# A decoder layer on one core: the quantised MLP's transposes by TensorE or by DMA

## The reference

```python
x = x + attn(ln(x))      # causal, 8 query heads, 2 key/value heads of 128 from latents of 32, softmax, wo
x = x + xattn(ln(x), ctx) # 16 heads of 16 over 77 keys, then relu(out @ W1 + b1) @ W2 + b2, 256 -> 512 -> 256
x = x + ffn(ln(x))       # 256 -> 1024 -> 256, quantised
...
scale = 127.0 / jnp.clip(jnp.max(jnp.abs(x), axis=-1, keepdims=True), EPS, None)   # per row, behind an rmsnorm
return jnp.clip(jnp.round(x * scale), -128, 127) / scale
...
scale = 1.0 / jnp.clip(jnp.mean(jnp.abs(w)), EPS, None)                            # one for the matrix
return jnp.clip(jnp.round(w * scale), -1, 1) / scale
...
h = gelu(bitlinear(x, w1, b1)); return bitlinear(h, w2, b2)
```

## Time and profile before

| | |
|---|---|
| three runs | 325.93, 327.07, 327.6 us; median 327.07 |
| the profiled execution | 328.01 us |
| its span (first to last instruction) | 326.2 us |
| mean granted TensorE clock | 0.99 |

### The profile page before, as it was taken

How to read it: one execution, slowest core, us unless ns; L and a number is a source line. 1 busy time by engine, 2 the same in 40 slices (tenths; PEclk the granted TensorE clock), 3 DMA queues, 4 the chain that set the end, 5 groups by cost and what they waited for, 6 DMA issues and landing times.

```text
span 326.2 us, 8843 instructions
## 1 busy us (share of the span) xinstructions
PE 304.7 (93%) x3174; PEld 242.7 (74%) x3174; DVE 271.5 (83%) x488; ACT 188.9 (58%) x367; POOL 162.0 (50%) x315
## 2 busy tenths in 40 slices
PE   0999889999999999999999999999999999999956
PEld 0578668688876897888877876888878786887634
DVE  1058987877878998999999989899999898899973
ACT  0434317335564674477746962798278636967762
POOL 7044158049118518740684078512760376457781
PEclk9999999999999999999999999999999999999987
DMA  7999000000000000001000000000010010000001
GB/s 204 342 368 301 3 1 2 2 2 0 2 4 2 1 2 2 1 2 34 0 3 20 4 16 0 2 2 1 3 34 2 2 34 2 18 1 2 19 33 64
DMA packets 11732, 12.54 MB, mean 38 GB/s; under 512 B 1639, under 2 KB 10729, under 8 KB 11690
## 3 DMA queue, kind: packets, MB, share of 16 engines
q1 hardware_dynamic: 10698, 11.66, 11.1%
q10 hardware_dynamic: 992, 0.33, 0.5%
HBM read 9.89 MB, written 2.10 MB: 37 GB/s over the span
## 4 chain that ended last, share of the span: by engine, by line
PE 66%; DVE 17%; POOL 7%; issue 5%; DMA 2%; ACT 1%; SPq 1%; DVEq 0%; POOLq 0%; ACTq 0%
PE bank L1872 7%; PE bank L1702 7%; PE bank L1782 6%; PE bank L1881 5%; PE bank L1849 5%; PE bank L1800 4%; PE bank L1708 3%; PE bank L1863 3%; PE quad L1762 3%; PE bank L1901 3%; PE quad L1839 3%; PE bank L1920 3%; PE bank L1696 2%; DVE c_nm L1251 2%; DVE c_s L1262 2%
## 5 line engine op out<-in xcount | busy, mean ns | idle before, releaser
L824 ACT ACTIVATE c_p<-bank 77x512 f32<-77x512 f32 x64 | 35.9, 589 | 34.6 <-PE bank L1849 34.3
L1849 PE MATMUL bank<-ident,c_s 128*77 128x128 f32 x256 | 37.1, 278 | 0.4 <-DVE a_y L1229 0.2
L579 POOL TENSOR_SCALAR f_s<-f_s 128x1 f32<-128x1 f32 x16 | 3.7, 229 | 66.8 <-ACT f_sq L870 53.9
L1849 PEld LDWEIGHTS bank<-ident,c_s 128*77 128x77 f32 x256 | 29.1, 147 | 4.9 <-issue 2.1
L800 ACT ACTIVATE a_p<-bank 128x512 f32<-128x512 f32 x48 | 26.9, 597 | 9.4 <-PE bank L1782 9.2
L1872 PE MATMUL bank<-c_y,xw_s 128*128 128x128 f32 x256 | 31.5, 276 | 0.2 <-DVE c_y L1281 0.2
L1872 PEld LDWEIGHTS bank<-c_y,xw_s 128*128 128x128 f32 x256 | 30.4, 192 | 1.4 <-issue 0.5
L1881 PE MATMUL bank<-xw_s,c_h 128*128 128x256 f32 x128 | 30.7, 383 | 0.0
L1251 DVE TENSOR_REDUCE c_nm<-quad 128x16 f32<-128x1232 f32 x16 | 22.9, 1431 | 4.8 <-PE quad L1839 4.8
L1320 DVE SCALAR_TENSOR_TENSOR f_h<-bank,f_s,fb_s 128x512 f32<-128x512 f32 x32 | 22.9, 739 | 3.7 <-PE bank L1901 3.3
L1881 PEld LDWEIGHTS bank<-xw_s,c_h 128*128 128x128 f32 x128 | 23.1, 190 | 3.4 <-issue 0.8
(11 more groups left out here) (138 smaller groups left out, 746.3 us busy)
## 6 DMA issues: line engine op xcount, KB each, us to landing
out<-f_o SPq DMA_DIRECT2D x16, 128.0 KB, 1.7
xres<-in_x SPq DMA_DIRECT2D x1, 1536.0 KB, 10.1
c_p<-in_wqT SPq DMA_DIRECT2D x2, 512.0 KB, 6.6
c_p<-in_wo SPq DMA_DIRECT2D x1, 1024.0 KB, 9.2
f_h<-in_fw1T SPq DMA_DIRECT2D x1, 1024.0 KB, 12.2
c_s<-in_fw2T SPq DMA_DIRECT2D x1, 1024.0 KB, 11.3
xw_s<-in_xw SPq DMA_DIRECT2D x2, 512.0 KB, 9.9
xres<-in_x SPq DMA_DIRECT2D x2, 256.0 KB, 5.4
```

Of the source, the lines that this page charges most:

```text
L824: nc.scalar.activation(c_p[0:M, :, qt * P:(qt + 1) * P].rearrange("p (c j g) t -> p c j g t", c=KC, g=Q2)[:, :, j, :, :], bank("xs", f"tr{ ...
L1849: last = nc.tensor.transpose(dst[0:M, g * P:(g + 1) * P], c_s[:, qt, j, g, :], ident[:, :])
```

## The change

The rounded tiles get a second copy in bfloat16, f_qb and f_hb, written by ScalarE (f1_qb, f2_hb) from SBUF with 1536 taken off. For elements 0 to 6 (BY_DMA = 7) SyncE then transposes them by DMAs into f_qT and f_hT, one DMA for each 128x128 block, 2 for a tile of f_q and 8 for a tile of f_hq; TensorE's and ScalarE's f1_qT and f2_hT are gone for these elements, and their fills of the rotating banks with them. For element 7 TensorE transposes the bfloat16 copy, and ScalarE evacuates it as before. SyncE's list has the transposes and the stores in an order written by hand. x of element 0 moves to ScalarE's queue; the context is loaded in two halves with a semaphore each, behind the first value weights. The tables and the calls of all engines are in a new order.

```diff
         def _(sp):
-            sp.dma_start(xres[:, 0:TT, :], xin[:, 0:TT, :]).then_inc(ld_x0, 16)
-            sp.dma_start(ctxa[:, :], ctxT[0:P, :]).then_inc(ld_ctx, 16)
-            sp.dma_start(ctxb[:, :], ctxT[P:P + CK, :]).then_inc(ld_ctx, 16)
-            sp.dma_start(xk_a[:, :], xk[0:P, :]).then_inc(ld_ctx, 16)
-            sp.dma_start(xk_b[:, :], xk[P:P + CK, :]).then_inc(ld_ctx, 16)
+            @element
+            def f1_qT(i, t):
+                sp.wait_ge(*f1.after("act", f"qb{t}", i))
+                for n in range(2 * t, 2 * t + 2):
+                    sp.wait_ge(*f1.after("pe", f"l1_{n}", i - 1))
+                for c in range(KC):
+                    sp.dma_start(f_qT[:, c, t * P:(t + 1) * P], f_qb[:, t, c * P:(c + 1) * P], transpose=True).then_inc(tr_q[t], 16)
+            @element
+            def f2_hT(i, t):
+                sp.wait_ge(*f2.after("act", f"hb{t}", i))
+                sp.wait_ge(*f2.after("pe", f"l2{t}", i - 1))
+                for c in range(FC):
+                    sp.dma_start(f_hT[:, t, c, :], f_hb[:, t, c * P:(c + 1) * P], transpose=True).then_inc(tr_h[t], 16)
...
             sp.dma_start(xv_a, xv[0:P, :]).then_inc(ld_xv, 16)
+            sp.dma_start(ctxa[:, 0:KH], ctxT[0:P, 0:KH]).then_inc(ld_ctx[0], 16)
             sp.dma_start(xv_b, xv[P:P + CK, :]).then_inc(ld_xv, 16)
+            sp.dma_start(ctxb[:, 0:KH], ctxT[P:P + CK, 0:KH]).then_inc(ld_ctx[0], 16)
+            sp.dma_start(xk_a[:, :], xk[0:P, :]).then_inc(ld_xk, 16)
+            sp.dma_start(xk_b[:, :], xk[P:P + CK, :]).then_inc(ld_xk, 16)
+            sp.dma_start(ctxa[:, KH:2 * KH], ctxT[0:P, KH:2 * KH]).then_inc(ld_ctx[1], 16)
+            sp.dma_start(ctxb[:, KH:2 * KH], ctxT[P:P + CK, KH:2 * KH]).then_inc(ld_ctx[1], 16)
             sp.dma_start(wkup_s[:, :], wkupT).then_inc(ld_up, 16)
...
-            for i in range(B):
-                for t in range(TT):
-                    sp.wait_ge(*f2.after("dve", f"out{t}", i))
-                    sp.dma_start(xout[:, i * TT + t, :], f_o[:, t, :]).then_inc(out_sem[t], 16)
...
+            f1_qT(2, 1)
+            f2_store(0, 0)
+            f2_hT(1, 1)
+            f2_store(0, 1)
+            f1_qT(3, 1)
+            f2_hT(1, 0)
+            f1_qT(3, 0)
...
+            f1_qT(6, 0)
+            f1_qT(6, 1)
+            f2_hT(5, 0)
+            f2_store(4, 0)
+            f2_hT(5, 1)
+            f2_hT(6, 0)
+            f2_store(4, 1)
+            f2_hT(6, 1)
+            f2_store(5, 0)
+            f2_store(5, 1)
...
         def _(act):
+            def transposed(done, n, i):
+                if i >= 0:
+                    act.wait_ge(done, 16 * n * min(i + 1, BY_DMA))
...
+            @element
+            def f2_hb(i, t):
+                act.wait_ge(*f2.after("dve", f"hq{t}", i))
+                transposed(tr_h[t], FC, i - 1)
+                if i > BY_DMA:
+                    act.wait_ge(*f2.after("pe", f"hT{t}", i - 1))
+                nc.scalar.activation(f_hb[:, t, :], f_hq[:, t, :], ACT.Copy, bias=-ROUND16).then_inc(f2.sem["act"], 1)
...
+            act.dma_start(xres[:, 0:TT, :], xin[:, 0:TT, :]).then_inc(ld_x0, 16)
...
             def f2_hq(i, t):
...
-                dve.wait_ge(*f2.after("pe", f"hT{t}", i - 1))
+                dve.wait_ge(*f2.after("act", f"hb{t}", i - 1))
...
             def f2_l2(i, t):
...
-                pe.wait_ge(*f2.after("act", f"hT{t}", i))
+                if i < BY_DMA:
+                    pe.wait_ge(tr_h[t], 16 * FC * (i + 1))
+                else:
+                    pe.wait_ge(*f2.after("act", f"hT{t}", i))
```

More of the change, by code:

```diff
@@ new lines, in _ @@
+            xp_q(4)
+            f2_hb(1, 1)
+            f1_gelu(2, 0)
+            f1_gelu(2, 1)
+            f1_pre(1)
+            sa_exp(5, "B", 0)
+            f2_ssq(2, 1)
+            sp_q(6)
+            xm_relu(3, 1)
+            sa_exp(5, "B", 3)
+            sa_exp(5, "B", 2)
+            xs_exp(4, 0, 3)
+            xs_exp(4, 0, 1)
+            f2_ssq(2, 0)
+            f2_hb(1, 0)
+            xs_exp(4, 1, 3)
+            xs_exp(4, 1, 1)
+            xs_exp(4, 1, 0)
+            sa_exp(5, "A", 0)
@@ L1044, in _ @@
+            sa_exp(5, "B", 1)
+            xs_exp(4, 1, 2)
+            xs_exp(4, 0, 2)
+            xs_exp(4, 0, 0)
+            f1_qb(3, 1)
+            sp_v(6)
+            f1_qb(3, 0)
+            sa_exp(6, "A", 1)
+            f1_pre(2)
+            f2_hb(2, 1)
+            xm_relu(4, 1)
+            f1_gelu(3, 1)
+            xm_relu(4, 0)
+            sp_xT(7)
             f1_pre(3)
-            xm_relu(3, 0)
-            xp_q(4)
-            f1_gelu(2, 0)
+            xp_xT(5)
+            f2_ssq(3, 1)
@@ L1147, in _ @@
-            f1_qT(6, 0)
+            xs_exp(7, 0, 1)
+            xs_exp(7, 1, 2)
             xs_exp(7, 1, 0)
-            xs_exp(7, 1, 2)
             xs_exp(7, 1, 1)
+            f1_qb(6, 0)
             xs_exp(7, 1, 3)
+            f1_pre(6)
+            f2_hb(5, 0)
+            f1_gelu(5, 1)
+            xm_relu(7, 0)
+            f1_qb(6, 1)
             f1_pre(7)
-            xm_relu(7, 0)
+            f2_ssq(5, 1)
             f1_gelu(6, 0)
+            xm_relu(7, 1)
+            f2_hb(5, 1)
@@ L1170, in _ @@
+            f2_hb(7, 1)
             f2_hT(7, 0)
@@ L1565, in _ @@
             xo_T(4, 1)
             xo_y(4, 1)
+            so_resid(5)
+            f1_q(3, 0)
+            xp_ln(5)
+            xo_y(4, 0)
+            f1_h(3, 3)
+            f2_hq(2, 0)
+            f1_h(3, 2)
+            sa_max(6, "B")
+            f2_hmax(3, 1)
+            xm_resid(4, 1)
+            f1_h(3, 1)
+            f1_h(3, 0)
+            sa_sub(6, "B", 0)
+            f1_ln(4, 1)
+            xm_resid(4, 0)
+            sa_sub(6, "B", 1)
+            f1_ln(4, 0)
+            f2_out(1, 0)
@@ L2151, in _ @@
-            xs_tr(3, 1, 2)
-            f1_qT(2, 0)
-            f2_l2(1, 0)
+            xs_tr(3, 0, 1)
+            xs_tr(3, 1, 2)
+            so_pv(4, 0)
+            so_pv(4, 1)
+            xo_pv(3, 0)
+            f2_l2(0, 0)
+            f2_l2(0, 1)
+            so_wo(4)
+            sp_k(6)
+            sa_tr(5, "A", 1)
+            xs_tr(3, 1, 3)
+            sa_scores(5, "B")
+            xs_tr(3, 1, 0)
+            xs_tr(3, 1, 1)
+            xm_w1(3, 0)
+            xp_xT(4)
+            f1_l1(2, 1)
@@ L2321, in _ @@
             f1_l1(7, 2)
-            f1_l1(7, 3)
-            f2_hT(6, 1)
             f2_l2(6, 0)
```

1696 lines of the change are left out of this document (826 added, 870 removed).

## The result

| | before | after |
|---|---|---|
| median of the runs | 327.26 us (4 runs) | 377.92 us (4 runs, 376.19 to 378.31) |
| profiled execution, span | 328.01, 326.2 us | 378.1, 376.3 us |
| end of the last xm_w2 (W) | 304.25 us | 327.89 us |
| from W to the end | 21.95 us | 48.4 us |

What follows compares the result with a forecast made beforehand. TensorE's work was taken to bound the middle, VectorE close behind, and a chain over four engines the tail. W at 299.95 plus 24.1 gave 324.05 us of span against 326.2, 324.9 in the median's terms; range 319 to 335.

Steps and rivals of the forecast that it cites:

- The pace of the queue: SyncE's queue: each 128x128 transposing DMA taken at 0.6 us, between 0.35 and 2.1, plus 2 us to the semaphore.
- Rival A: Tail: SyncE's transposes run back to back and set the end; 332 us of span at 1.0 us each, 339 at 1.3; chance 0.30.
- In the middle this is hidden: Middle: an element needs 12 us of SyncE's queue plus waits, against 41 us, an eighth of the span.
- they stop fitting at about 1.3: Elements 0 to 4: at about 1.3 us a transpose the queue no longer fits; f2_hT(2,0) comes some 6 us late.
- my own formula: Tail, x us a transpose, over 0.71: last f_hT data at W-0.9+24x+2, end 7.0 us later.
- TensorE, W 4.3 us earlier: Before W: 6.1 us less TensorE work, 70% of it arriving, so W at 299.95 instead of 304.25.
- ScalarE, 1.06 + 0.2 us: Tail: element 7's added conversions cost 1.06 us for the last f2_hb and about 0.2 for that tile's f1_qb.
- The start, 0: Start: TensorE may begin some 2 us earlier but waits at wqT; gain 0, with +1 and -1.5 us as ends.
- Rival B: Middle: VectorE takes over, only 2 us of 6.1 arrive, W 302.3; no change, 327.2 us; chance 0.15.
- C: Whole kernel: all 6.1 us arrive, W at 298.1, pace near 0.5, start 1.5 us earlier; 320.6 us; chance 0.20.

Runs made afterwards that it cites:

- the first five elements: Changed kernel with the tiles of elements 5 and 6 transposed by TensorE again, those of elements 0 to 4 by 100 DMAs: 348.96 us, 1.0663 of before.
- all by TensorE, bfloat16 copies: Changed kernel's loads, bfloat16 copies and order, with all transposes on TensorE and none by DMA: 336.88 us, 1.0292 of before.
- one DMA a tile: Changed kernel with one transposing DMA for each tile instead of two and eight, 28 in all: 318.89 us, 0.9740 of before.
- element 7 in float16: Changed kernel with 28 DMAs, one for each tile, and element 7 transposed by TensorE without bfloat16 copies: 317.89 us, 0.9707 of before.

## Why the prediction was wrong

*The pace of the queue, "I take 0.6 us": this step failed.* It measured 1.23 us for one and 1.27 us from one to the next. I had bounded it by 0.35 and 2.1 us, which holds it, and then went to the lower end because DMAs of one queue overlap. They do here too: each lands 2.3 us after its issue, at a pace of 1.27. But overlap in flight says nothing of how long an instruction holds the queue, and that is the pace. The trace before had only plain DMAs, and an operation of another kind between bounds six times apart should have stood in the middle of them. That the middle, 1.2, would have been right is luck; but my own sum turned from faster to slower at 0.76, low between the bounds, and that called for more than 0.30 on A. The Trainium skill ("VectorE: DVE Perf Modes", The three transpose paths) has 1309 ns for a 128x128 transpose by the crossbar DMA. That was near the measured 1.23 us, but here the price is one for an instruction, of 16 rows or of 1024 columns alike, and not one for a block. The Trainium skill ("Advanced Engine Details and Errata", X-Bar Transpose (TRN2)) has transposing DMAs as fast as regular ones. For the time in the queue that doesn't hold, 1.23 us against 0.60.

*Rival A, "the queue's pace ends the tail", 339 at 1.3.* The right mechanism, with 0.30, and its price too small by 37 us. At 1.27 my own formula gives 299.95 - 0.9 + 24 x 1.27 + 2 + 7.0 = 338.5; the span is 376.3. Of the missing 37.8 us, 27.9 lie ahead of W (327.89, not 299.95) and 9.9 in the tail. In the tail I let f2_hT(5,1) start at W-0.9 with a queue that was free; it starts at 334.16, W+6.3, because f2_hT(5,0) was late too (7.2 us). The queue then runs until 366.24, 32.1 us for 24 transposes and a store instead of 30.5 (1.6), and the end comes 10.1 us after that, not 9.0 (1.1), at a granted clock of 0.55.

*"In the middle this is hidden", "they stop fitting at about 1.3".* This was the second failed step, and it fails at a pace that I did price. I compared an element's 20x with an eighth of the span, 41 us. But the queue's work begins at 97.8 us, and elements 2 to 6 follow each other in 33 us (their first xm_w2 start at 151.81 and 283.47 before): 26.6 us of queue in 33, in order, behind waits for copies and for stores. That needs no full queue to be late, as the 12 us of the first five elements show. The step that I had named, f2_hT(2,0) "some 6 us late" at 1.3, was right: TensorE waited 6.53 us for it. But at that pace I named this step alone, and gave it no price in the sum. f1_qT(3,0) behind f2_hT(1,0), which I had found to fit at 0.6, cost TensorE 4.18 us at 211.07, and f1_qT(5,1) another 10.96 at 312.82. I also left out what a late step does in a fixed order: everything behind it on TensorE comes later, the next copies start later, and the granted clock stands at 0.86 and less. That is how I read the 9 us of W that no wait for a DMA covers; no run separates the parts.

*TensorE, W 4.3 us earlier, "I take 70%".* The mechanism was right and too small. Where the queue doesn't hinder, W is at 290.30, 14.0 us earlier. From "all by TensorE, bfloat16 copies" to one DMA a tile it moves by 15.6 us (305.93 to 290.30). Of such a difference between two single executions some 1 to 2 us can be the start (the first xm_w2 begins between 78.18 and 80.27 us in these kernels; counted from there it is 14.5), so the +0.6 of the new order and the +1.1 of the copies can't be told from nothing. I had priced the transposes by what they hold in the chain, 0.45 and 0.11 us, 7.8 us in all. In a stretch of their own they last 0.61 and 0.27 us (14 x 0.88 = 12.3), and TensorE's busy time fell by 13.8 us (305.5 to 291.7). About all of it arrived, where I took 70% of too small a price. Whether the four banks and ScalarE's evacuations, which I put at nothing, were worth something as well, no run tells.

*ScalarE, 1.06 + 0.2 us.* This term was for element 7 alone, and the kernel with element 7 in float16 is its test: 1.0 us in the medians, 1.1 in the two tails (25.6 and 24.5), though the intervals overlap. The 5.7 us by which the copies cost "all by TensorE" more (331.14 to 336.88) are another price: there all eight elements have the copy and keep the evacuation, a step more in series. In the changed kernel the copies of elements 0 to 6 stand in place of evacuations, which I had let cancel; no run tests that by itself.

*The start, 0.* Right: the loads by themselves give 0.9988. TensorE's first matmul came 2.1 us earlier, the first pro_wq step 1.4 us, and nothing was left of it. *Rival B* (VectorE takes over) is excluded by the 318.89 us; *C* (all of it arrives, 320.6) comes near what the kernel does when the queue is relieved, 318.89, but by other parts: W 7.8 us earlier than C had it, a tail of 25.6 us instead of 23.2, and no gain at the start.

By the forecast's own test ("wrong if the eight DMAs take 7 us or more, if TensorE waits for f_hT already in the middle, or if W stays above 302") it failed on all three: 10.0 us, waits from 158.98 us on, 327.89.

## What to carry to other kernels

Work moved to a queue isn't free because the DMA engines idle: count the instructions, multiply by the time that one holds the issuing engine, and compare with the pace at which the queue's own stage runs, not with the span over the number of elements. Then look for entries of the queue that wait for data while the next one's data are there. If the kind of instruction isn't in the trace, measure it or stand in the middle of its bounds; and if the price turns out to be per instruction, make the instruction larger before dropping the idea. Here the change lost 15% with 140 instructions and gained 2.6% with 28 that do the same.

## What the hardware showed that I had not expected

- A transposing DMA held SyncE's queue for 1.23 us with 16, 64 or 128 rows and for 1.24 us with 1024 columns; a plain one of 128x128 for 0.60 us.
- One transposing DMA turned a tile of 128x1024 into eight transposed blocks, landing 3.1 us after its issue, against 10.0 us of queue and 2.3 us to landing for eight.
- The f2_l2 of eight matmuls took 1.04 us in a busy stretch and 1.87 us after TensorE had idled for 4.4 to 8.9 us in the tail, where the granted clock was 0.69 (300 to 350 us) and 0.55 (from 350 us). The wait just before isn't all of it: behind 3.9 us of idling they took 1.87 us in the changed kernel (272.58) and 1.03 us in the one with the first five elements (273.09). Nor is a lower clock in the tail all due to the DMAs: without any wait for one it was 0.80 there (one DMA a tile), against 0.58 in the changed kernel.
